# Attention inside a fused layer: GpSimd adds the probabilities of four pairs of key blocks, sums inverted on 16 columns, another order in the slots

## The reference

```
xn = layernorm(x)
Q, K, V = proj(xn, Wq), proj(ctx, Wk), proj(ctx, Wv)        # 16 heads of 32
attn = softmax(Q K^T / sqrt(32)); out = (attn V) Wo^T + bo
x = x + tanh(g_xattn) * out
x = x + tanh(g_ffn) * moe(layernorm(x))                     # 8 experts, top 2, capacity 1.2
```

## Time and profile before

| | |
|---|---|
| device time, median of 3 | 1835.09 us |
| profiled execution: its time / its span | 1835.47 / 1833.8 us |
| PE, DVE, ACT, POOL busy, share of the span | 95%, 59%, 44%, 24% |
| a batch in the loop, first output projection to the next | 109.7 us |
| granted TensorE clock over the span | 0.974 of full |
| TensorE busy in `with_ones`, 1024 matmul instructions | 136.4 us |

### The profile page before, as it was taken

One profiled execution on the slowest core, in us unless ns is written; L12 is line 12 of the kernel. 1 busy time (PEld: TensorE's weight loads), 2 busy tenths in 40 slices (PEclk: granted clock), 3 DMA queues, 4 the chain that ended last, 5 costly groups with the idle time before them and its releaser, 6 DMA issues.

```text
span 1833.8 us, 29428 instructions
## 1 busy us (share of the span) xinstructions
PE 1735.7 (95%) x10322; PEld 820.0 (45%) x10322; DVE 1077.9 (59%) x2087; ACT 803.3 (44%) x1092; POOL 435.1 (24%) x424
## 2 busy tenths in 40 slices
PE   7999999999999999999815999999999999999998
PEld 4324243242423324243203747565565747566563
DVE  6777867677776777867677625435262534424231
ACT  4553735547364553735421616244252615344240
POOL 2322434224343322431211121112121121102101
PEclk9999999999999999999956999999999999999999
DMA  6343263334435433243022362626354262626312
GB/s 224 104 92 117 71 160 115 97 116 103 136 98 132 143 92 115 76 115 109 30 110 81 105 160 87 181 50 180 75 140 122 97 165 86 159 63 174 78 47 28
DMA packets 214606, 203.17 MB, mean 111 GB/s; under 512 B 121812, under 2 KB 162912, under 8 KB 210456
## 3 DMA queue, kind: packets, MB, share of 16 engines
q1 hardware_dynamic: 193432, 181.80, 33.0%
q0 software_dynamic: 21120, 20.67, 6.5%
HBM read 134.57 MB, written 43.63 MB: 97 GB/s over the span
## 4 chain that ended last, share of the span: by engine, by line
PE 84%; DVE 9%; issue 3%; ACT 2%; POOL 1%; DMA 1%; SPq 0%; DVEq 0%; ACTq 0%; POOLq 0%
PE psum L1552 23%; PE psum L1528 21%; PE psum L1354 7%; PE psum L1361 6%; PE psum L1345 6%; PE psum L1335 6%; PE psum L1325 6%; PE psum L1443 4%; PE psum L1372 3%; DVE mx L925 2%; DVE reached L1077 1%; DVE x2hl L997 1%; DVE x2hl L999 1%; DVE stats L877 1%; DVE x2n L884 1%
## 5 line engine op out<-in xcount | busy, mean ns | idle before, releaser
L1552 PE MATMUL psum<-w,hT 128*128 128x512 f16 (+1 forms) x1920 | 415.7, 379 | 0.0
L1528 PE MATMUL psum<-xgT,w 128*128 128x308 f16 (+1 forms) x3072 | 409.9, 294 | 0.8 <-DVE xgT L1178 0.8
L925 DVE TENSOR_REDUCE mx<-psum 128x1 f32<-128x512 f32 x512 | 330.2, 684 | 105.6 <-PE psum L1335 103.9
L1528 PEld LDWEIGHTS psum<-xgT,w 128*128 128x128 f16 x3072 | 297.5, 97 | 109.8 <-DVE xgT L1178 1.1
L779 ACT ACTIVATE pt<-psum 128x1024 f32<-128x1024 f32 x256 | 260.7, 1024 | 133.9 <-PE psum L1345 133.9
L1552 PEld LDWEIGHTS psum<-w,hT 128*128 128x128 f16 (+1 forms) x1920 | 199.3, 104 | 213.8
L851 ACT ACTIVATE h<-psum,b1c 128x308 f32<-128x308 f32 (+1 forms) x256 | 118.4, 514 | 341.9 <-PE psum L1528 341.5
L1199 DVE TENSOR_TENSOR hT<-h,hT 128x615 f16<-128x615 f32 x128 | 102.6, 801 | 211.8 <-ACT hT L854 211.8
L672 POOL DMA_INDIRECT out_dram<-y,idx_now x40 | 87.8, 2194 | 498.6 <-DVE y L1231 312.0
L1228 DVE SCALAR_TENSOR_TENSOR y<-psum,b2b 128x512 f32<-128x512 f32 (+1 forms) x40 | 27.7, 692 | 270.4 <-PE psum L1552 270.4
L1325 PE MATMUL psum<-actT,wT 128*128 128x512 f16 x768 | 179.2, 381 | 2.0 <-DVE wT L912 2.0
(11 more groups left out here) (187 smaller groups left out, 1504.9 us busy)
## 6 DMA issues: line engine op xcount, KB each, us to landing
stage<-in_L_ffn_W_dram SPq DMA_DIRECT2D x62, 1024.0 KB, 5.7
stk<-qk_rows SPq DMA_DIRECT2D x192, 128.0 KB, 2.5
qk_rows<-qks SPq DMA_DIRECT2D x64, 256.0 KB, 2.5
xin<-in_x_dram SPq DMA_DIRECT2D x8, 1024.0 KB, 5.4
cin<-in_ctx_dram SPq DMA_DIRECT2D x8, 1024.0 KB, 7.5
xres<-in_x_dram SPq DMA_DIRECT2D x8, 1024.0 KB, 5.6
out_dram<-xres SPq DMA_DIRECT2D x32, 256.0 KB, 2.1
x_split<-x2hl SPq DMA_DIRECT2D x32, 256.0 KB, 2.3
```

What stands on the lines that cost most here:

```text
L925: v.reduce_max(mx[:, KT * t + qt:KT * t + qt + 1], ps, AX.X).then_inc(read, 1)
L1528: mm = t_.matmul(psum[:, (2 * m + ch) % 4, 0:c1 - c0], w1[:, wp, kt, m * P:(m + 1) * P], xgT[:, KT * xp + kt, c0:c1], start=(kt == 0 and ( ...
L1552: mm = t_.matmul(psum[0:rows, Y_BANK[i], :], hT[:, hp, k, c * P:c * P + rows], w2[:, wp, k, :], start=(k == 0 and (hp, wp) == (0, 0)), sto ...
```

## The change

Three things are changed.

1. For units 0 to 7 POOL adds the probabilities of the second unit of a pair to those of the first, in place, and TensorE multiplies the sum with ones once for each pair; units 8 to 15 are multiplied one by one. A table says in which slot each of the 12 products stands. The probabilities get five buffers for a unit in place of two, three of them tensors that are idle by then (`qk32`, `x2nT`, `x2n`); ACT waits for `sums_done` of the unit five before.
2. The sums are inverted after a 32x32 transpose (each head's 32 equal rows become columns), on 16 columns, and transposed back. This is one block of three instructions for a group.
3. In slots below 16 PE runs `with_values` last and `with_ones` in the middle. DVE normalises the next `x` in slots 5 and 6 in place of POOL; POOL computes its inverse deviations earlier; the adds to `xres` now stand between the second and third pair on POOL. SP's list is the same.

The diff, cut to its core:

```diff
-RECIP_SLOT = ((11, 12, 13, 14), (15, 16, 16, 17), (19, 19, 20, 20), (23, 23, 23, 23))
-GROUP_NORM = [slots[-1] for slots in RECIP_SLOT]
+PAIRS, PT_UNITS = 4, 5
+SUMS = {10: (("pair", 0),), 12: (("pair", 1),), 14: (("pair", 2),), 16: (("pair", 3),), 17: (("unit", 8),),
+        18: (("unit", 9), ("unit", 10)), 19: (("unit", 11),), 20: (("unit", 12), ("unit", 13)),
+        21: (("unit", 14),), 22: (("unit", 15),)}
+GROUP_NORM = [16, 18, 20, 23]
+GROUP_SPLIT = [17, 19, 21, 23]
+X_NORM_SLOT = (5, 5, 6, 6)
...
+        pt_units = ([pt[:, 2 * i:2 * i + 2, :, :] for i in range(2)]
+                    + [a.rearrange("p (a b) s -> p a b s", b=2) for a in (qk32[:, :, :], x2nT[:, :, :], x2n[:, :, :])])
...
-                pool.wait_ge(mrow_ready, NG * b + 3)
-                pool.wait_ge(xres_in, 16 * b + 16)
-                pool.wait_ge(tgbo_ready, 1)
-                for tt in range(KT):
-                    g.tensor_tensor(xres[:, tt, :], xres[:, tt, :], tgbo[:, :], ALU.add).then_inc(xres_biased, 1)
+                for p in range(PAIRS):
+
+                    if p == 2:
+                        pool.wait_ge(xres_in, 16 * b + 16)
+                        pool.wait_ge(tgbo_ready, 1)
+                        for tt in range(KT):
+                            g.tensor_tensor(xres[:, tt, :], xres[:, tt, :], tgbo[:, :], ALU.add).then_inc(xres_biased, 1)
+                    if p % 2 == 0:
+                        pool.wait_ge(mrow_ready, NG * b + (p // 2 + 2))
+                    pool.wait_ge(pv_done, UNITS * b + (2 * p + 1))
+                    for hf in range(2):
+                        copied(pool, use, ("ST", 2 * p + 1, hf), b)
+                        for j in range(2):
+                            into = pt_units[2 * p % PT_UNITS][:, hf, j, :]
+                            g.tensor_tensor(into, into, pt_units[(2 * p + 1) % PT_UNITS][:, hf, j, :],
+                                            ALU.add).then_inc(pair_added, 1)
...
-                            act.wait_ge(pv_done, UNITS * b + max(u - 1, 0))
+                            if u < PT_UNITS:
+                                act.wait_ge(sums_done, SUM_COUNT * b)
+                                act.wait_ge(qk_split, NQ * b + NQ)
+                            else:
+                                act.wait_ge(sums_done, SUM_COUNT * b + (sum_of_unit(u - PT_UNITS) + 1))
...
+                    v.transpose(turned_sums[:, :], sums).then_inc(sums_turned, 1)
+                    dve.wait_ge(sums_turned, NG * b + g + 1)
+                    own = mx[:, NT // 2 * g:NT // 2 * g + NT // 2]
+                    v.reciprocal(own, turned_sums[:, :].rearrange("p (c k) -> p c k", k=32)[:, :, 0:1].rearrange(
+                        "p c k -> p (c k)")).then_inc(sums_inverted, 1)
+                    dve.wait_ge(sums_inverted, NG * b + g + 1)
+                    v.transpose(osum[:, g % 2, 1, :].rearrange("p (c k) -> p c k", k=32),
+                                own.rearrange("p (c o) -> p c o", o=1).to_broadcast((P, NT // 2, 32))).then_inc(rinv_done, 1)
...
+                        for tt in range(KT):
+                            if t == X_NORM_SLOT[tt]:
+                                normalise(0, tt, KT * b + (KT + tt), xin[:, tt, :], xn[:, tt, :], xn_ready)
...
+                def with_ones(s):
+                    for kind, n in SUMS.get(s, ()):
+                        i = SUM_ORDER.index((kind, n))
...
+                        if kind == "pair":
+                            pe.wait_ge(pair_added, 4 * PAIRS * b + (4 * n + 4))
+                        src = pt_units[(2 * n if kind == "pair" else n) % PT_UNITS]
...
                     less_maxima(u, 0)
+                    if s < UNITS:
+                        with_ones(s)
+                        scores(s, 2)
+                    less_maxima(u, 1)
+                    scores(s, 3)
...
                     with_values(s - LAG_C)
-                    scores(s, 2)
-                    less_maxima(u, 1)
-                    scores(s, 3)
-                    if 0 < s - LAG_C < UNITS and (s - LAG_C) % 4 == 0:
-                        pe.wait_ge(sums_ready, (NG - 1) * b + (s - LAG_C) // 4)
-                    with_ones(s - LAG_C)
+                    if s >= UNITS:
+                        with_ones(s)
```

More of the change, by code:

```diff
@@ L50 @@
 GROUP_END = [LAG_C + 4 * g + 3 for g in range(NG)]
-RECIP_SLOT = ((11, 12, 13, 14), (15, 16, 16, 17), (19, 19, 20, 20), (23, 23, 23, 23))
-GROUP_NORM = [slots[-1] for slots in RECIP_SLOT]
+PAIRS, PT_UNITS = 4, 5
+SUMS = {10: (("pair", 0),), 12: (("pair", 1),), 14: (("pair", 2),), 16: (("pair", 3),), 17: (("unit", 8),),
+        18: (("unit", 9), ("unit", 10)), 19: (("unit", 11),), 20: (("unit", 12), ("unit", 13)),
+        21: (("unit", 14),), 22: (("unit", 15),)}
+SUM_ORDER = [term for slot in sorted(SUMS) for term in SUMS[slot]]
+SUM_COUNT = len(SUM_ORDER)
+GROUP_SUMS = [[i for i, (kind, n) in enumerate(SUM_ORDER) if n // (2 if kind == "pair" else 4) == g] for g in range(NG)]
+SUMS_END = [max(slot for slot in SUMS for term in SUMS[slot] if SUM_ORDER.index(term) in GROUP_SUMS[g]) for g in range(NG)]
+GROUP_NORM = [16, 18, 20, 23]
+GROUP_SPLIT = [17, 19, 21, 23]
+X_NORM_SLOT = (5, 5, 6, 6)
 def chunk_rows(c):
@@ L62, in later_qk, with sum_of_unit @@
     return [QK_FIRST + j for j, slot in enumerate(QK_SLOT) if slot == s]
+def sum_of_unit(u):
+    return SUM_ORDER.index(("pair", u // 2) if u < 2 * PAIRS else ("unit", u))
 def later_v(s):
@@ L582, in batch @@
                     if i == QK_FIRST + 2:
+                        if not last:
+                            for tt in range(KT - 1):
+                                inverse_deviation(0, tt, KT * b + (KT + tt))
                         pool.wait_ge(mrow_ready, NG * b + 1)
+                    if i == QK_FIRST + 3 and not last:
+                        inverse_deviation(0, KT - 1, KT * b + (2 * KT - 1))
                     pool.wait_ge(qk32_ready, NQ * b + i + 1)
@@ L966, in batch @@
                     for g in range(NG):
-                        for quarter in range(4):
-                            if t == RECIP_SLOT[g][quarter]:
-                                reciprocals(g, (quarter,))
+                        if t == GROUP_NORM[g]:
+                            inverse_sums(g)
                     if t in GROUP_NORM:
                         g = GROUP_NORM.index(t)
-                        dve.wait_ge(rinv_done, KT * (NG * b + g + 1))
+                        dve.wait_ge(rinv_done, NG * b + g + 1)
+                        if g < NG - 1:
+                            dve.wait_ge(osum_ready, (NG - 1) * b + g + 1)
                         dve.wait_ge(a_hi, NG * b + g)
@@ L1353, in with_values @@
                             h = 4 * g + j
[L1354 to L1359 removed]
+                            last = t_.matmul(psum[32 * j:32 * j + 32, 6, :], v32[:, kt, HD * h:HD * h + HD],
+                                             pt_units[u % PT_UNITS][:, j // 2, j % 2, :], start=(kt == 0), stop=(kt == KT - 1))
+                        last.then_inc(pv_done, 1)
+                def with_ones(s):
+                    for kind, n in SUMS.get(s, ()):
+                        i = SUM_ORDER.index((kind, n))
+                        terms = next(t for t in GROUP_SUMS if i in t)
+                        gr = GROUP_SUMS.index(terms)
+                        if i == terms[0] and gr > 0:
+                            pe.wait_ge(sums_ready, (NG - 1) * b + gr)
+                        if kind == "pair":
+                            pe.wait_ge(pair_added, 4 * PAIRS * b + (4 * n + 4))
+                        src = pt_units[(2 * n if kind == "pair" else n) % PT_UNITS]
                         for j in range(4):
[L1361 to L1363 removed]
+                            last = t_.matmul(psum[32 * j:32 * j + 32, 7, :], ones32[:, :], src[:, j // 2, j % 2, :],
+                                             start=(i == terms[0]), stop=(i == terms[-1]))
+                        last.then_inc(sums_done, 1)
                 def values(tt, halves=range(2)):
```

41 lines of the change are left out of this document (13 added, 28 removed).

## The result

The changed kernel takes 1842.42 us, the median of five runs (1841.59 to 1844.29), against 1835.09 (five runs). The ratio is 1.0041, 95% interval 1.0028 to 1.0054. It is 0.4% slower where I had forecast 1832.4, 0.1% faster, and it lies above the range of 1821 to 1841.

What follows compares the result with a forecast made beforehand. TensorE was taken to bound the kernel. First batch -4.8, seven batches -7 x 1.2, seven clock falls +7 x 1.5: -2.7 us from 1835.1 gives 1832.4 us; range 1821 to 1841.

Steps and rivals of the forecast that it cites:

- the price of a low clock: Half clock around the stop in seven batches: at most about 1.7 us each, taken as 1.5, 10.5 in all.
- what the slots give in seven batches: Gain in slots 7 to 22 before the clock's price: 7 x 1.2 us.
- The place and the cause of the stop: TensorE stands 5.0 us before the third pair's product, while GpSimd's bias adds wait for the xres load, then the pair's adds.
- The fall of the clock in all seven stops and not in the first batch: Clock falls from 2.4 to 1.2 GHz in nearly all seven stops of 5 us, not in the one of 1.4.
- 1.2 us a batch: Gain per batch with the stop, before the clock's price: 1.0 us in slots 7 to 16, 0.2 in 17 to 22.
- TensorE without waits: Slots 7 to 22 at TensorE's own pace, 2.84 us without a ones product: gain 7 us a batch, 56 in all.
- The first batch: No stores ahead of the xres load, so TensorE stops only 1.4 us; this batch gains 4.8 us.
- the clock didn't hold: Rival for the stops: the clock holds or falls in few of them, -13.2 us, 1821.9; chance 0.20.
- the load came no sooner: Rival at the third pair: xres lands sooner, no wait for it, -38 us, 1797; chance 0.05, shared with no stop.
- longer adds or a longer low clock: Slower case: GpSimd's adds at 1.47 in place of 1.24 lengthen the stop, +14.7 us, 1847; chance 0.15 with longer low clock.
- A rule that speaks against the change: Eight adds between load and product: at VectorE's 0.69 in place of GpSimd's 1.24 the stop would be 4.4 us shorter.
- What costs nothing: Inverted sums ready at 464.3, wanted at 466.0; ScalarE's exponentials fit the slots; inverse deviations lie in GpSimd's idle time.

Runs made afterwards that it cites:

- The filled stop: The changed kernel with 19 more matmuls on TensorE ahead of the wait for the third pair, in batches 1 to 7: 1826.21 us.
- the bias adds last: The changed kernel with GpSimd's four bias adds to xres moved behind the fourth pair: 1798.58 us.
- five pairs: The changed kernel with bias adds behind the fourth pair and fourth mrow, plus a fifth pair (units 8 and 9, product in slot 18): 1816.81 us.
- the inverse alone: The kernel before with only the transposed inverse of the sums, in the slot of the fourth reciprocal piece: 1841.76 us.
- the load first: The changed kernel with the load of xres issued on SP ahead of the four stores of the split rows: 1844.13 us.
- the stop half filled: The changed kernel with 9 more matmuls on TensorE ahead of the wait for the third pair, in batches 1 to 7: 1833.4 us.

## Why the prediction was wrong

Two terms of the sum failed, by about as much each: the price of a low clock (15.0 us where I had 10.5) and what the slots give in seven batches (3.6 where I had 8.4). With one of them alone as forecast the sum would have stayed inside the range.

*The place and the cause of the stop* were right. The times were close. From the start of slot 7 the second mrow came at 5.5 (forecast 5.2), the load landed at 19.3 (18.8) and the third pair's product started at 29.25 (28.9; the terms, 18.8 + 2 x 4.97, add to 28.7). TensorE stood 4.3 us for GpSimd (5.0), since it was itself at 24.9 there and not at 23.9. GpSimd's add of a pair took 1.24, as priced. Slots 17 to 22 took 17.6. Ahead of the other pairs TensorE waited 0.2 at most, and in the first batch 0.3 where I had 1.4.

*The fall of the clock in all seven stops and not in the first batch* was right.

*The first step that failed is "The price is at most about 1.7 each ... I take 1.5, for 7 x 1.5 = 10.5 us".* The filled stop puts it at 2.1 each, 15.0 in all. I had one row to read a price from, 12.14 against 10.47, a low stretch of 3.4 us, and took it as the upper bound. The three stretches of that length did cost 1.7. In four of seven batches the stretch was twice as long and cost 2.5. The clause "where it falls early, part of the low time lies in the stop itself, and then it is nearer to 1.0" went the wrong way: where it fell early the stretch was the long one, and 5.2 to 6.0 us of it lay behind the stop.

*The second is "1.2 us a batch".* With the clock held, seven batches give 767.5 - 763.9 = 3.6 us, 0.5 each. In the filled stop's rows the product starts 0.4 later than in my working (29.3 against 28.9), and from there to the end of slot 16 it takes 9.0 us where I had 8.6. Of the second 0.4 slot 15 has 0.3: the slot of "2.84" takes 3.15, as said above. I had asked whether VectorE has room for four maxima in a slot, and not whether the third score has to wait for the first of them. Slots 11 and 13 have the same wait, which is why TensorE reached the third pair 1.0 late; there GpSimd's chain hid it. It also makes "TensorE without waits", 7 us a batch, too much: with the bias adds last it is 4.6.

So the sum over seven batches is -3.6 + 15.0 = +11.4 where I had -8.4 + 10.5 = +2.1. With the first batch at -3.8 that is +7.6, and the medians differ by 7.3.

*The first batch* took 5.4 us less up to its output projection (123.5 against 128.9), where I had 4.8. 1.6 of that are the first 48 projections, which ran at the full clock in this one execution (10.52 against 12.14) and lie outside the change. That leaves 3.8. It can account for a profiled span that grew by 6.1 only while the median grew by 7.3.

*The rivals.* None of the rivals happened: the clock didn't hold, the adds took 1.24 beside the other engines, and the load came no sooner. The case called slower, "longer adds or a longer low clock", had the right second half, but I had put no price on it. Its first half is real elsewhere: with five pairs an add took 1.52 beside VectorE's operations with two SBUF inputs.

*"A rule that speaks against the change"*, GpSimd's add at 1.24 where VectorE's takes 0.69, was not tried by itself. The experiments show what its price meant: the eight adds and the load were the whole chain to the product, and with four of the eight behind it TensorE doesn't wait there.

*What costs nothing*: true for the inverse in the changed kernel (block 1.7, the last group's result in time). It isn't true of the same block put into a slot with maxima, as the inverse alone showed, and the sentence didn't say that its place carried it.

## What to carry to other kernels

Work that is taken off the busiest engine and given to an idle one can be worth nothing if it stands in that engine's list behind something unrelated that waits for a DMA: here moving four adds behind the pairs in the list was worth 44 us, six times what the whole change had lost. Price a new stop of TensorE with its clock, and with a long low stretch, not the shortest one in the trace. When work leaves a list, ask what it covered: here the third score's wait for a maximum. And ask of every instruction moved later who else waits for that engine next, as the five pairs showed.

## What was not expected of the hardware

The clock's low stretches had two lengths, 3.4 and 6.8 us. In the changed kernel and with the load first the long ones stood behind stops of 4.3 us and more, and the short ones behind stops of up to 4.24; but with the stop half filled a long one followed a stop of 2.38. What sets the length is not shown. Stops of 3.8 us and more dropped the clock every time (14 of 14 in these two kernels). Stops of 2.2 to 2.8 us dropped it in three of six with the stop half filled, and stops of 2.4 in three of seven with five pairs; one of 1.5 and those of 1.2 did not. TensorE's stop of 2.0 at the start, which is the same in all twelve kernels, dropped it in nine of the twelve profiled executions (the 48 projections behind it took 12.1 to 12.2 us) and not in three (10.52). The Trainium skill ("TensorE: Matmul & The Clock Gate", section "HAM oscillation — how this bites in real kernels") says that waits between bursts of matmuls cost the warm clock again and again; the trace agrees, seven times in seven at 3.8 to 5.2 us.

VectorE's instructions of 16 columns with operands in SBUF took 0.80 and 1.20 us in place of 0.17 and 0.18 beside GpSimd's adds. The Trainium skill ("SBUF — State Buffer", section "SBUF: two separate sides") says that the two engines share one pair of ports, and that whichever takes the pair first keeps it for its whole instruction while the other waits. The rows are in line with that, since neither instruction is longer by more than one add of 1.24. With the bias adds held back until the fourth mrow, and nothing else changed, both instructions took 0.17 again.

19 matmuls a batch that compute nothing of use made the kernel 16 us faster: with them the clock stayed at 1.00 through attention.
